# Decoder layer: attention scores from plain fp32 queries and keys on four row groups of TensorE, in place of high and low parts stacked through DRAM

## The reference

```python
q = heads(hidden_states @ Wq)            # (b, 16, 512, 32), fp32
k = heads(hidden_states @ Wk)
scores = jnp.einsum('bhqd,bhkd->bhqk', q, k) / jnp.sqrt(jnp.float32(D))
attn = jax.nn.softmax(scores, axis=-1)
std = jnp.einsum('bhqk,bhkd->bhqd', attn, v)
...
qa = _affinities(q, positions, directions, scales, ds)   # also from q and k
ka = _affinities(k, positions, directions, scales, ds)
```

## Time and profile before

| | us |
|---|---|
| median of 3 runs (1487.76 to 1492.16) | 1489.92 |
| the profiled execution's own time | 1490.79 |
| its span in the profile | 1489.0 |
| PE busy (matmul) | 1213.1 (81%) |
| DVE busy | 1205.5 (81%) |
| ACT busy | 765.7 (51%) |
| chain that ended last: DVE, PE, issue, ACT, DMA | 36%, 32%, 9%, 5%, 5% |

### The profile page before, as it was taken

One profiled execution on the slowest core, in us unless ns is written; L12 is line 12 of the kernel. 1 busy time (PEld: TensorE's weight loads), 2 busy tenths in 40 slices (PEclk: granted clock), 3 DMA queues, 4 the chain that ended last, 5 costly groups with the idle time before them and its releaser, 6 DMA issues.

```text
span 1489.0 us, 14210 instructions
## 1 busy us (share of the span) xinstructions
PE 1213.1 (81%) x4698; PEld 562.5 (38%) x4698; DVE 1205.5 (81%) x1457; ACT 765.7 (51%) x1118; POOL 164.5 (11%) x211
## 2 busy tenths in 40 slices
PE   4573858687689997897899897888899888877996
PEld 3342323232245543333345433333355433333453
DVE  5878898888879997879789996888799996887323
ACT  6765534435367743545467653555477534452331
POOL 1000111001111120100101121000111210001001
PEclk8865878777969999889889998899799997988898
DMA  6853795556329869443249686362279593651231
GB/s 189 283 172 113 169 252 144 114 127 142 58 91 260 229 154 255 111 117 85 66 126 274 159 229 180 87 165 46 66 207 274 115 241 103 147 130 29 64 99 43
DMA packets 112667, 220.20 MB, mean 148 GB/s; under 512 B 14561, under 2 KB 25313, under 8 KB 112593
## 3 DMA queue, kind: packets, MB, share of 16 engines
q1 hardware_dynamic: 88608, 142.85, 31.2%
q0 software_dynamic: 18432, 67.12, 23.4%
q10 hardware_dynamic: 5552, 9.31, 1.8%
HBM read 122.37 MB, written 29.62 MB: 102 GB/s over the span
## 4 chain that ended last, share of the span: by engine, by line
DVE 36%; PE 32%; issue 9%; ACT 5%; DMA 5%; SPq 2%; DVEq 0%; POOL 0%; ACTq 0%; POOLq 0%
DVE ST L878 13%; PE ps L1289 6%; DVE ST L870 5%; PE ps L1480 5%; DVE MX L934 5%; PE ps L1272 4%; DMA qk_parts<-PT 3%; PE ps L1424 3%; PE ps L1440 2%; PE ps L1381 2%; DVE QAK L1100 2%; PE ps L1350 2%; DVE QS L1087 2%; PE ps L1240 2%; DVE ST L881 1%
## 5 line engine op out<-in xcount | busy, mean ns | idle before, releaser
L878 DVE TENSOR_TENSOR_SCAN ST<-dA,ST 128x1024 f32<-128x1024 f32 x128 | 292.9, 2288 | 9.4 <-ACT dA L574 6.7
L1480 PE MATMUL ps<-V,GU 128*128 128x512 f16 x1024 | 238.5, 388 | 5.6 <-DVE V L1074 5.6
L934 DVE TENSOR_REDUCE MX<-ps 128x1 f32<-128x512 f32 x256 | 165.3, 686 | 77.2 <-PE ps L1272 76.6
L490 POOL DMA_DIRECT2D YA<-ST x128 | 109.4, 855 | 979.1 <-DVE ST L881 931.0
L574 ACT ACTIVATE dA<-DL,Aneg 128x511 f32<-128x511 f32 x256 | 168.3, 712 | 58.5 <-DVE ST L878 54.2
L711 ACT ACTIVATE PT<-ps 128x1024 f32<-128x1024 f32 x128 | 126.4, 1021 | 123.9 <-PE ps L1381 123.2
L1272 PE MATMUL ps<-KS,QS 96*128 96x512 f32 x256 | 126.3, 554 | 74.1 <-DVE MX L934 48.3
L881 DVE TENSOR_TENSOR ST<-ST,BC 128x1024 f32<-128x1024 f32 x128 | 156.8, 1225 | 4.4
L870 DVE TENSOR_TENSOR ST<-DU,BC 128x1024 f32<-128x1024 f32 x128 | 155.9, 1218 | 0.6 <-issue 0.4
L1480 PEld LDWEIGHTS ps<-V,GU 128*128 128x128 bf16 x1024 | 97.1, 100 | 140.9 <-issue 31.3
L1440 PE MATMUL ps<-QS 128*128 128x512 f32 x512 | 142.8, 422 | 2.5 <-DVE QS L1087 1.7
(11 more groups left out here) (229 smaller groups left out, 1550.2 us busy)
## 6 DMA issues: line engine op xcount, KB each, us to landing
YA<-ST POOLq DMA_DIRECT2D x128, 512.0 KB, 7.3
BC<-bc_rows SPq DMA_DIRECT2D x64, 512.0 KB, 7.8
GU<-gu_tiles SPq DMA_DIRECT2D x64, 256.0 KB, 4.5
QS<-proj_tiles SPq DMA_DIRECT2D x64, 256.0 KB, 4.1
qk_parts<-PT ACTq DMA_DIRECT2D x32, 256.0 KB, 4.4
qk_parts<-PT SPq DMA_DIRECT2D x32, 256.0 KB, 5.2
QS<-qk_parts SPq DMA_DIRECT2D x32, 256.0 KB, 4.2
KS<-qk_parts SPq DMA_DIRECT2D x32, 256.0 KB, 5.8
```

Of the source, the lines that this page charges most:

```text
L878: nc.vector.tensor_tensor_scan(flat, dA[:, a, :, :].rearrange("p e s -> p (e s)"), flat, 0.0, ALU.mult, ALU.add).then_inc(s_scan, 1)
L934: nc.vector.tensor_reduce(MX[:, j % 2, qt, h:h + 1], ps[:, n % 2, :], AX_X, ALU.max).then_inc(s_mx, 1)
L1480: last = mm(ps[:, f % F_RING, :], GU[:, t % GU_RING, k, m * P:(m + 1) * P], XHL[:, z, k, :], start=(k == 0 and z == 0), stop=(k == KT - 1 ...
```

## The change

`qk_parts`, the stacks, the high and low parts and their semaphores go. ScalarE copies each unit once as fp32 into QK (z, j) and squares it into PT; a head stays in its own 32 partitions. Scores are fp32 matmuls of 32 rows with `tile_position=(32h, 0)`, so that four heads (or two) use four (or two) row groups of the array. The maxima of four heads come in one group of four matmuls into banks 0 to 3 and are reduced by one 128x2048 reduction to four columns; a group waits for the reduction of the group before. The bias is a second matmul of one row (fp32r, `one_row` and BR), accumulated on the scores. All score pairs now use banks 4 and 5, so a pair waits for the exponential of the pair before. The splat products wait for all units of a kind and run on four column groups at once. The rings BC and WP go from 3 and 4 to 2.

```diff
@@ buffers
-        BC = sb("BC", [P, BC_RING, 2, S])
+        BC = sb("BC", [P, 2, 2, S])
-        QS = [sb(f"QS{i}", [P, HG, S], F32R) for i in range(2)]
-        KS = [sb(f"KS{i}", [P, HG, S], F32R) for i in range(2)]
-        HL = QS[1]
+        QK = sb("QK", [P, 2, NG, S])
+        HL = sb("HL", [P, 4, S], F32R)
-        WP = QS[0]
+        WP = sb("WP", [P, 2, H], F32R)
@@ ScalarE, fill unit u (the high part, its DMA and their waits go)
-                    nc.scalar.copy(PT[:, 0, u % 2, :], bank)
-                    nc.scalar.square(PT[:, 0, 2 + u % 2, :], bank).then_inc(s_q32, 1)
+                    nc.scalar.copy(QK[:, z, j, :], bank)
+                    nc.scalar.square(PT[:, u // HG, u % HG, :], bank).then_inc(s_q32, 1)
@@ VectorE
+            def max_groups(b, j, lo, hi):
+                for g in range(lo, hi):
+                    dve.wait_ge(s_xs, KT * NG * b + KT * j + g + 1)
+                    since(dve, s_tm, NG * b + j)
+                    nc.vector.tensor_reduce(MX[:, g, 0:P:D], ps[:, 0:HG, :], AX_X, ALU.max).then_inc(s_mx, 1)
@@ TensorE, max_scores
+                for g in range(lo, hi):
+                    n = KT * j + g
+                    if n == 0:
+                        pe.wait_ge(s_ev, 2 * KT * (b + 1))
+                    else:
+                        pe.wait_ge(s_mx, KT * NG * b + n)
...
+                    for h in range(HG):
+                        rows = slice(D * h, D * h + D)
+                        last = mm(ps[:, h, :], QK[rows, 0, j, g * P:(g + 1) * P], QK[rows, 1, j, :],
+                                  start=True, stop=True, tile_position=(D * h, 0))
+                    last.then_inc(s_xs, 1)
@@ TensorE, a pair of scores
+            def score_pair(b, j, kt, p):
+                for h in (2 * p, 2 * p + 1):
+                    rows = slice(D * h, D * h + D)
+                    mm(ps[:, score_bank(h), :], QK[rows, 1, j, kt * P:(kt + 1) * P], QK[rows, 0, j, :],
+                       start=True, stop=False, tile_position=(D * h, 0))
+                for h in (2 * p, 2 * p + 1):
+                    row = slice(D * h, D * h + 1)
+                    last = mm(ps[:, score_bank(h), :], one_row[row, :], BR[row, j % 2, :],
+                              start=False, stop=True, tile_position=(D * h, 0))
+                last.then_inc(s_s, 1)
@@ the waits of a pair in the slots
-                                pe.wait_ge(s_exp, 2 * KT * NG * b + (s if one_pair else s - 1))
+                                pe.wait_ge(s_exp, 2 * KT * NG * b + s)
@@ where the groups of maxima stand (one line of the table)
+        GROUPS = {0: (1, 2, 3, 4, 4), 1: (0, 2, 3, 4, 4), 2: (0, 1, 3, 4, 4), 3: (0, 0, 0, 0, 0)}
@@ SyncE: load_stack goes, WP waits for the tile two before
+                    if t >= 2:
+                        sp.wait_ge(s_dn, NT * b + t - 1)
+                    sp.dma_start(WP[:, t % 2, :].bitcast(F32), proj_tiles[t]).then_inc(s_wp[t % 2], 16)
```

More of the change, by code:

```diff
@@ L158, in decoder_layer @@
         s_gu = [sem(f"s_gu{i}") for i in range(GU_RING)]
-        s_wp = [sem(f"s_wp{i}") for i in range(WP_RING)]
+        s_wp = [sem(f"s_wp{i}") for i in range(2)]
         s_gp, s_up, s_sg, s_h, s_hh, s_hl, s_sqa, s_ssq, s_acc, s_dn = (sem(n) for n in (
@@ L166, in decoder_layer @@
             "s_xd", "s_xdc", "s_bcw", "s_dt", "s_abs", "s_rel", "s_spe", "s_ln", "s_dl", "s_du", "s_ya"))
-        s_bc = [sem(f"s_bc{i}") for i in range(BC_RING)]
+        s_bc = [sem(f"s_bc{i}") for i in range(2)]
         s_dA, s_dBu, s_scan, s_prod = (sem(n) for n in ("s_dA", "s_dBu", "s_scan", "s_prod"))
@@ L285, in decoder_layer @@
         ROWS1 = (2, 3, 0, 1)
[L286 to L293, removed]
+        UNITS = ((0, 0), (0, 1), (1, 0), (1, 1), (2, 0), (2, 1), (3, 0), (3, 1))
+        FILL_BANKS = (0, 2, 1, 0, 2, 1, 0, 1, 6, 7, 4, 5, 6, 7, 6, 7)
+        GU_USES = NT // 2
         def gu_loaded(b, t):
@@ L333, in load_bc @@
             def load_bc(bb, n):
[L335 to L338, removed]
+                if type(bb) is not int or bb > 0 or n >= 2:
+                    sp.wait_ge(s_prod, half(bb, n - 2, 1) + 1)
                 sp.wait_ge(s_bcw, 16 * bb + 16)
@@ L347, in store_bc @@
                 sp.dma_start(bc_rows[bb], XD[DR:DR + 2 * DS, :]).then_inc(s_bcw, 16)
[L349 to L363, removed]
-                                     parts.rearrange("(h p) a s -> (p a) h s", p=D)).then_inc(s_stack[i][pair], 16)
-                        sp.dma_start(dst[2 * D:3 * D, heads, :].bitcast(F32),
-                                     parts[:, z, :].rearrange("(h p) s -> p h s", p=D)).then_inc(s_stack[i][pair], 16)
             def load_next_bc(b, halves):
@@ L376, in attention_phase @@
                     load_ctx(b + 1)
-                for r in range(2 * KT):
+                for r in range(4 * KT):
                     load_next_bc(b, fill_halves(r, first))
[L379 to L383, removed]
-                    load_next_bc(b, fill_halves(2 * KT + u, first))
                 for j in range(NG + 1):
-                    for c, chunk in enumerate(slot_halves(j, first)):
-                        if c == KT - 1 and j + 2 < NG:
-                            load_stack(b, j + 2)
+                    for chunk in slot_halves(j, first):
                         load_next_bc(b, chunk)
@@ L548, in _ @@
             link(nc.gpsimd.memset(mhalf[:, :], -0.5))
-            for i in range(2):
-                link(nc.gpsimd.memset(KS[i][3 * D:3 * D + 1, :, :].bitcast(F32), 1.0))
+            link(nc.gpsimd.memset(one_row[:, :].bitcast(F32), 1.0))
+            link(nc.gpsimd.memset(MX[:, :, :], 0.0))
             for h in range(HG):
@@ L1398, in attention_phase @@
                                 prep_context(b + 1)
-                        for p in range(2):
-                            if kt > 0:
-                                values(b, j, kt - 1, 6 + p)
-                            max_scores(b, j + 1, cuts[2 + p], cuts[3 + p])
-                        if j + 1 < NG and kt == KT - 2:
+                        if j + 1 < NG and kt == KT - 1:
                             transpose_max(b, j + 1)
```

206 lines of the change are left out of this document (75 added, 131 removed).

## The result

The changed kernel is slower: 1520.7 us, the median of four runs (1502.2 to 1531.1), against 1488.8 for the kernel before (1486.6 to 1492.2); the ratio is 1.013 (95% interval 1.010 to 1.017), lower than that of the medians because it counts only the two quickest runs of the changed kernel, the others lying over 1.5% above its fastest. I had forecast 1470. The profiled execution took 1525.3 us.

The account below looks back on a forecast made before the run. Neither DVE nor PE alone bounds the kernel (both busy 81%); the work changes hands by stages, DVE bounding batch 0. From 1490.8, -40 and +21 for the clock give 1471 profiled, 1470 median; likeliest 1450 to 1486, 8-in-10 range 1442 to 1540.

Parts of the forecast that it names:

- the term for the clock: Slots, all batches: five products a batch at half clock after waits, 5.3 us a batch, 21 in all (0 to 60).
- my sum without the clock: Whole kernel: batch 0 -17, batches 1 and 2 -7 each, batch 3 -9, together -40 us.
- Rival (1): Slots: small gaps of PE waiting put the clock at 0.75 instead of 0.89; 60 us lost, 1530, slower; chance 0.25.
- The fill: Stretch before the first pair, batches 1 to 3: 19 us shorter, about 54.6 us long in batch 1.
- The slots at full clock: Batches 1 and 2: four slots of 28, 26, 30.5, 36, sum 120.5, a loss of 12 us; batch 3 becomes 110.
- Rival (2): Row groups don't overlap: a group of maxima takes 3.5 us, a pair 2.0; time 1650; chance 0.12.
- Batch 0: Bound by DVE: 20 us less idle, work down 5.5 and 5, PE's slots 12 longer; taken as 17 us gained.
- The rings: BC and WP with fewer buffers: loads have 9.5 us to land; cost 0, for BC at most 2 us a batch.

Follow-up runs that it names:

- the second profile: Control: the changed kernel run again with no edit, against the kernel before; 1510.3 us (1500.3 to 1526.5), ratio 1.012.

## Why the prediction was wrong

**The step that failed** is the term for the clock: "I allow five such products a batch, 5 x 1.06 = 5.3, 21 in all (0 to 60)." The slots of 28, 26, 30.5 and 36 us were laid out at full clock, so this term had to hold all that half clock costs in them. In batch 1 a clock of 0.80 over 142 us is (1 - 0.80)/0.5 = 40% of the time at half, 57 us, and work done in them would take 28 less. The same for batches 2, 3 and 0 (0.76, 0.85, 0.89) gives 35, 18 and 15: some 97 in place of 21, and 78 in the second profile. It is an upper bound, since waits lie in it.

For batches 1 to 3 the account closes so: forecast 120.5 + 120.5 + 110 + 16 = 367 us of slots, measured 412, of which 82 are half clock in place of 16, and 330 the rest in place of 351. So the clock's term was 66 us too low and the slots at full clock 21 too high. With batch 0 (below), 9 us short of its forecast, that is the 54 between 1471 and 1525.

Two things were in my rows already. The kernel before loses 66 us by the same measure (0.89 and 0.79 in the earlier trace rows), and 39 of them in batches 1 to 3, where I allowed 16; I compared slots at full clock with slots that had their half clock in them. And I took half clock as one product behind a wait, but in the earlier trace rows the values at 633.39 are at half 6 us after the wait at 627.31. What came on top is the change's own: its narrow products, as the runs show that change the rows of the same products (0.69 on 32 rows, 0.89 on 97 and 96) or of the same bias (0.91 over 128 rows, 0.80 and 0.87 on one; 0.93 with wide work, 0.61 with narrow). The run with 128 rows in all products has slots at 0.93 to 1.00 and is 37 us under the kernel before, where my sum without the clock was -40; its pair and group cost about the same (1.0 and 1.05 us, against 1.19 and 0.96), so the agreement is fair, not exact.

Rival (1) was right in its place, the slots' clock, and near in its time (1530), and I gave it 0.25. Its mechanism is not what the runs show: it put the clock down to small waits, of which PE had fewer in these slots than before (11.4 us in all against 16.7 in batch 1), and not to the products. That its 1530 lies so near to 1521 is in part luck, since it stood on slots that were too long at full clock.

**The fill**: forecast 54.6 us, measured 55.1, 55.0 and 55.1 in batches 1 to 3, with no wait for a DMA. This step was right; PE is busy 53.6 of the 55.1 us in batch 1 and DVE 50.8, so it is PE that bounds it now.

**The slots at full clock**: forecast 28, 26, 30.5, 36. Measured where the clock was near full: slot 1 24.1 (0.99), slot 3 36.1 (0.95). Slot 2 had 33.2 at 0.90, slot 0 32.8 at 0.79. An exponential starts 690.80 - 689.40 = 1.40 after its pair in slot 3 (1.5 forecast), the cycle is 691.88 - 689.40 = 2.48 (2.55). Groups 0.96 (1.1), pair 1.19 to 1.29 (1.2). Rival (2), no overlap, is refuted by these. The estimate from the Trainium skill, page "TensorE: Matmul & The Clock Gate", part on packing small matmuls, was 1.14 for a group; the trace has 0.96, a little better.

**Batch 0**: forecast -17, came as -2.5 (fill -11.6, slots +9.1). This is a second miss, and not the clock's, which rose in these slots from 0.79 to 0.89. I took 20 us off DVE's idle time, because 77.2 us stood ahead of the reductions in the whole run. In batch 0 it was 14.1; the view of DVE's waits there, before and after:

```profile
DVE MX L934 <- PE ps L1272: 14.1, 16, 2.4
```

```profile
DVE MX L873 <- PE ps L1201: 18.3, 8, 7.3
```

DVE's work fell by 8.5 us (10.5 forecast), its idle time rose from 27.3 to 33.4. The fewer reductions wait for PE's maxima as long in all as the single ones did; what makes PE late there no run separates. With 128 rows in all products the wait is 15.4 and batch 0's fill and slots are 86.0 + 131.1, 10 less than before and still 7 short of the 17. The reductions themselves are 2.29 us (2.27 forecast) and 146.5 together (145):

```profile
L873 DVE TENSOR_REDUCE MX<-ps 128x4 f32<-128x2048 f32 x64 | 146.5, 2290 | 97.6 <-PE ps L1201 97.6
```

**The rings**: DVE never waits for BC, as said. For WP, PE waited 9.4 us in all, and the feed-forward stretches are as long as before.

## What to carry to other kernels

Price a tiled matmul twice: by its time at full clock, and by the rows that it leaves unused, because in a stretch that is bound by TensorE its clock decides. When you lay out a stretch at full clock, take the half clock out of what you compare it with, and allow at least as much as the old kernel has. Before you split work into row groups, try a run of the old kernel with the same products cut to fewer rows: one edit showed here which way the clock would go, though it fell further (0.69) than in the rewrite. Where a short operand can be padded with zero rows at no cost in time, pad it: that gave 0.7% in the kernel before.

## What the runs showed of the hardware

- Granted clock in the slots of batch 1, by what the products of queries and keys use. In the order before: scores 128 and maxima 96 rows 0.92, 97 and 96 rows 0.89, 32 rows of the same products 0.69. In the new order: 128 rows 0.96 (0.88 without the bias), row groups with two records 0.80 and 0.87 in two profiles, with the bias over 128 rows 0.91; with one record 0.66, with yet more one-row matmuls 0.61, with the bias over 128 rows 0.93. Each time that the same products or the same bias were given other rows, the clock went with them; between the two orders it need not (0.79 before and 0.89 after in batch 0).
- Four fp32 matmuls of 32 rows and 512 columns on four row groups take 0.96 us, where one of 128 rows takes 0.87. Two on two row groups take the same 0.96.
- Two one-row matmuls on the row groups of the pair before overlap with it (0.23 added for both); over 128 rows they do not (0.66 added).
